# A new order of every engine's calls in the block loop of a fused attention and expert kernel

## The reference

```
nq = layernorm(x)
q, k, v = nq @ wq + bq, ctx @ wk + bk, ctx @ wv + bv          # per head
out = (q @ k.T / sqrt(8)) @ v                                # = q @ (k.T @ v) / sqrt(8)
x = x + softmax(out, axis=-1) @ wo.T + wo_b                   # softmax over the 8 of a head
t = rms_norm(layernorm(x)) * norm_w
probs = softmax(t @ gate.T);  top 2 of 8 experts, weights normalised
h1 = t @ w1.T + 2 * (t @ a1.T) @ b1.T                         # a1, b1, ... are the expert's
h3 = t @ w3.T + 2 * (t @ a3.T) @ b3.T
act = silu(h1) * h3
x = x + sum_e weight_e * (act @ w2.T + 2 * (act @ a2.T) @ b2.T)
```

## Time and profile before

| | |
|---|---|
| time of 3 runs, median (lowest to highest) | 325.44 us (325.40 to 326.32) |
| the profiled execution: time, and its span | 322.72 us, 320.9 us |
| granted TensorE clock over the span | 0.992 of full speed |
| busy share: PE, PEld, DVE, ACT, POOL | 92%, 74%, 73%, 59%, 59% |
| HBM read, written | 12.07 MB, 2.14 MB |

### The profile page before, as it was taken

One profiled execution on the slowest core, in us unless ns is written; L12 is line 12 of the kernel. 1 busy time (PEld: TensorE's weight loads), 2 busy tenths in 40 slices (PEclk: granted clock), 3 DMA queues, 4 the chain that ended last, 5 costly groups with the idle time before them and its releaser, 6 DMA issues.

```text
span 320.9 us, 4516 instructions
## 1 busy us (share of the span) xinstructions
PE 294.3 (92%) x1485; PEld 237.1 (74%) x1485; DVE 233.7 (73%) x621; ACT 187.9 (59%) x309; POOL 188.5 (59%) x171
## 2 busy tenths in 40 slices
PE   6768999879999999999999999999999979996993
PEld 5545778658788778878788778878888767885782
DVE  3879877695679766895679767895579766973364
ACT  2456956358657577448657576548647455654511
POOL 3472469727981589527981689527941688136910
PEclk9999999999999999999999999999999999999996
DMA  5720020200201021200211020200010000200000
GB/s 166 260 66 2 1 67 0 100 0 3 98 21 79 0 66 35 99 0 5 96 30 72 0 65 35 99 1 0 35 66 35 0 1 34 102 0 0 33 2 33
DMA packets 7223, 14.50 MB, mean 45 GB/s; under 512 B 1824, under 2 KB 3104, under 8 KB 7200
## 3 DMA queue, kind: packets, MB, share of 16 engines
q1 hardware_dynamic: 6624, 13.62, 12.7%
q10 hardware_dynamic: 576, 0.59, 0.6%
HBM read 12.07 MB, written 2.14 MB: 44 GB/s over the span
## 4 chain that ended last, share of the span: by engine, by line
PE 35%; DVE 24%; POOL 23%; issue 12%; ACT 2%; DMA 2%; ACTq 0%; DVEq 0%; POOLq 0%
PE h_ps L617 15%; PE h_ps L603 6%; POOL um_lo L1608 5%; POOL heads L1601 4%; POOL v_lo L1623 3%; POOL masks L1614 3%; POOL v L1619 3%; DVE act_first L1315 3%; DVE z_lo L1325 3%; DVE scaled L1307 2%; PE odd_ps L692 2%; DVE masks L1239 2%; PE even_ps L452 2%; PE z_ps L452 2%; PE b_ps L452 2%
## 5 line engine op out<-in xcount | busy, mean ns | idle before, releaser
L617 PE MATMUL h_ps<-um_lo,b_hi 128*128 128x512 f32 x128 | 50.9, 398 | 2.3 <-DVE um_lo L1288 2.1
L961 ACT ACTIVATE silu<-h_ps 128x512 f32<-128x512 f32 x64 | 38.2, 597 | 24.7 <-PE h_ps L617 23.3
L617 PE MATMUL h_ps<-um_hi,b_hi 128*128 128x512 f32 x128 | 51.1, 399 | 1.0 <-DVE act_first L1301 0.9
L617 PE MATMUL h_ps<-um_hi,b_lo 128*128 128x512 f32 x128 | 49.9, 390 | 0.0
L1301 DVE TENSOR_TENSOR act_first<-silu,h_ps 128x512 f32<-128x512 f32 x32 | 21.9, 686 | 36.5 <-ACT silu L961 25.2
L1601 POOL TENSOR_TENSOR heads<-e_o,rec_o 128x512 f32<-128x512 f32 (+1 forms) x9 | 14.8, 1642 | 55.9 <-DVE rec_o L1178 55.9
L1630 POOL TENSOR_TENSOR scaled<-act_second,ratio 128x512 f32<-128x512 f32 x24 | 31.0, 1291 | 11.0 <-DVE act_second L1301 10.9
L1301 DVE TENSOR_TENSOR act_second<-silu,h_ps 128x512 f32<-128x512 f32 x32 | 21.6, 679 | 16.9 <-PE h_ps L617 13.4
L617 PEld LDWEIGHTS h_ps<-um_lo,b_hi 128*128 128x128 f32 x128 | 24.0, 188 | 10.4 <-DVE um_lo L1288 4.6
L953 ACT CAST um_hi<-umf 128x1024 fp32r<-128x1024 f32 x14 | 14.7, 1053 | 28.3 <-DVE umf L1282 28.3
L603 PE MATMUL h_ps<-t_hi,w_hi 128*128 128x512 f32 x64 | 28.5, 446 | 0.9 <-DVE e_o L1171 0.3
(11 more groups left out here) (275 smaller groups left out, 788.4 us busy)
## 6 DMA issues: line engine op xcount, KB each, us to landing
chosen<-choice_dram SPq DMA_DIRECT2D x7, 768.0 KB, 3.9
x_in<-in_x_dram SPq DMA_DIRECT2D x7, 256.0 KB, 2.9
ctx_in<-in_ctx_t_dram SPq DMA_DIRECT2D x7, 256.0 KB, 3.2
out_dram<-y SPq DMA_DIRECT2D x7, 256.0 KB, 2.0
act_second<-in_hidden_w_dram SPq DMA_DIRECT2D x1, 512.0 KB, 4.3
act_second<-in_lora_w_dram SPq DMA_DIRECT2D x1, 512.0 KB, 5.1
v_parts<-in_down_w_dram SPq DMA_DIRECT2D x1, 512.0 KB, 6.1
attn_sb<-in_attn_w_dram SPq DMA_DIRECT2D x1, 260.5 KB, 5.1
```

The lines of the kernel that those rows point to most:

```text
L617: mm = nc.tensor.matmul((h1_ps, h3_ps)[s][n % 2][:], b13[w][:, s, c * P:(c + 1) * P], um[k][m][:, s, :], start=False, stop=(i == 2), skip_ ...
L961: nc.scalar.activation(silu[:, n % SILU_RING, :], h1_ps[n % 2][:], ACT.Silu).then_inc(silu_done.sem, 1)
```

## The change

The change gives the four engine lists of the loop a new order. The lists ahead of the loop and behind it stay, as do all calls, their waits, and SP's list. One constant goes with it: the first of the `w2_product` calls in a loop iteration is now that of quarter 1, since it is the one that clears the bank.

The diff of the loop, in the order PE, ACT, DVE, POOL:

```diff
-W2_ORDER = (0, 1, 2, 3)
+W2_ORDER = (1, 0, 2, 3)
...
                 hidden(b, 0)
+                hidden(b, 1)
                 turn_heads(b + 1)
-                hidden(b, 1)
+                hidden(b, 2)
                 project(b + 1)
-                if early:
-                    turn_x(b + 2)
-                hidden(b, 2)
+                hidden(b, 3)
                 if early:
                     keys_values(b + 2, 0)
+                    turn_x(b + 2)
                 b2_product(b - 1)
-                hidden(b, 3)
+                hidden(b, 4)
+                if early:
+                    queries(b + 2)
+                tail(b - 1)
                 if early:
                     keys_values(b + 2, 1)
-                    queries(b + 2)
-                tail(b - 1)
-                hidden(b, 4)
                 turn_tok(b + 1)
+                hidden(b, 5, (1,))
                 if early:
                     keys_times_values(b + 2)
+                gate(b + 1)
                 hidden(b, 5, (0,))
-                gate(b + 1)
                 if early:
                     attention_out(b + 2)
-                hidden(b, 5, (1,))
                 hidden(b, 6)
                 hidden(b, 7)
+                lora_in(b + 1, 0)
+                w2_product(b, 1)
+                w2_product(b, 0)
                 a2_product(b, 0, 1)
+                a2_product(b, 1, 1)
+                a2_product(b, 2, 1)
                 a2_product(b, 0, 0)
-                a2_product(b, 1, 1)
+                lora_in(b + 1, 1)
                 a2_product(b, 1, 0)
-                w2_product(b, 0)
-                w2_product(b, 1)
-                lora_in(b + 1, 0)
-                lora_in(b + 1, 1)
-                a2_product(b, 2, 1)
                 a2_product(b, 2, 0)
                 w2_product(b, 2)
-                a2_product(b, 3, 1)
                 a2_product(b, 3, 0)
                 w2_product(b, 3)
+                a2_product(b, 3, 1)
...
                 silu_step(b, 0)
+                silu_step(b, 1)
                 heads_turned(b + 1)
+                v_high(b - 1)
+                silu_step(b, 2)
                 if early:
                     normal_x(b + 2)
-                silu_step(b, 1)
-                v_high(b - 1)
+                silu_step(b, 3)
                 if early:
                     x_turned(b + 2)
-                silu_step(b, 2)
+                b_high(b, 0)
                 output_t(b - 1)
-                silu_step(b, 3)
                 normal_tok(b + 1)
+                silu_step(b, 4)
                 if early:
                     queries(b + 2)
-                b_high(b, 0)
-                silu_step(b, 4)
                 tok_turned(b + 1)
...
                 b_high(b, 1)
+                if early:
+                    exp_o(b + 2)
                 b_high(b, 2)
                 z_high(b, 1)
                 z_high(b, 2)
-                exp_gap(b + 1)
-                exp_ratio(b + 1)
-                if early:
-                    exp_o(b + 2)
                 um_high(b + 1, 0)
                 um_high(b + 1, 1)
+                exp_ratio(b + 1)
+                exp_gap(b + 1)
...
                 act_step(b, 0)
                 act_step(b, 1)
+                act_step(b, 2)
                 residual(b + 1)
                 moments_x1(b + 1)
-                act_step(b, 2)
+                act_step(b, 3)
+                if b + 3 < BLOCKS:
+                    moments_x(b + 3)
                 if early:
                     keys_values(b + 2, 0)
-                act_step(b, 3)
+                finish(b - 1)
                 if early:
                     keys_values(b + 2, 1)
-                finish(b - 1)
-                if b + 3 < BLOCKS:
-                    moments_x(b + 3)
+                    mask_ktv(b + 2)
+                tok_low(b + 1)
                 act_step(b, 4)
-                tok_low(b + 1)
-                if early:
-                    mask_ktv(b + 2)
                 top_logits(b + 1)
                 choose(b + 1)
-                act_step(b, 5)
                 if early:
                     top_of_o(b + 2)
+                act_step(b, 5)
+                act_step(b, 6)
+                if early:
                     shift_o(b + 2)
-                act_step(b, 6)
                 act_step(b, 7)
+                b_low(b, 1)
                 scale_last(b)
                 total(b, 2)
                 total(b, 3)
-                b_low(b, 1)
+                mask(b + 1, 0)
+                z_low(b, 1)
                 b_low(b, 2)
-                z_low(b, 1)
                 z_low(b, 2)
-                mask(b + 1, 0)
+                mask(b + 1, 1)
                 mask_u(b + 1, 0)
-                mask(b + 1, 1)
+                mask_u(b + 1, 1)
+                um_low(b + 1)
                 if early:
                     sum_exp(b + 2)
-                um_low(b + 1)
-                mask_u(b + 1, 1)
-                first_weight(b + 1)
                 v_part(b, 0)
                 v_part(b, 1)
+                first_weight(b + 1)
...
+                v_sum(b - 1)
                 scale_mask(b)
-                v_sum(b - 1)
                 v_low(b - 1)
+                scale_step(b, 0)
                 rstd_x1(b + 1)
-                scale_step(b, 0)
                 scale_step(b, 1)
+                b_low(b)
                 total_first(b)
-                b_low(b)
                 z_low(b)
                 if b + 3 < BLOCKS:
-                    rstd_x(b + 3)
                     ctx_low(b + 3)
                 scale_step(b, 2)
+                if b + 3 < BLOCKS:
+                    rstd_x(b + 3)
+                um_low(b + 1)
                 if early:
                     norm_heads(b + 2)
-                um_low(b + 1)
```

## The result

The changed kernel takes 313.85 us (median of 4 runs, 312.93 to 314.08) against 325.42 us (4 runs, 325.16 to 326.32) in the same comparison: a ratio of 0.9634, 95% interval 0.9608 to 0.9661. The profiled execution took 314.08 us, with a span of 312.3 us.

A forecast was written before the change was run, and what follows sets the result against it. PE was taken as the bound, busy 92% of the span. Gains of 5.6 us up to X of block 6, 1.7 in block 6 and 1.2 in block 7, together 8.6, gave 325.44 - 8.6 = 316.8 us, range 314.8 to 322.0.

The forecast's parts named there:

- PE alone, without waits, needs 34.7 us, between 34.5 and 34.9: PE's time per loop iteration, X (third product of hidden step 0) to X: 35.89 - 1.20 + 0.2 - 0.2 us.
- the three waits of 1.20 us: PE's idle times per iteration before X, behind X and before b2_product, 1.20 us together, predicted to go.
- The +0.2 for two more places with a slow first product: On PE, two more groups of small products alone between hidden steps, about 0.1 us each per iteration.
- The -0.2 for slow starts: On PE, slower products behind the waits, predicted to be recovered: up to 0.2 us each, 0.2 per iteration in the sum.
- the new wait at 1.0 us and the late chain at 0.5: Block 6 losses: turn_tok waits about 1.0 us for the normalised tokens; DVE's chain is late by 0.5 us.
- The base: The profiled execution, 322.72 us before, would take 314.1; the median of runs stood 2.72 us above it.
- DVE's chain: On DVE, from key-value product through choice and attention maximum to um_lo, ending 34.7 us behind X, level with PE.
- Rival 1: In blocks 1 to 4 DVE's cast of the choice loses to POOL's ctx_lo, 1.2 us later: 321.4 us, chance 0.26.
- Rival 2: Small POOL operations, rstd_x's root, also hold DVE, 1.0 us in each of blocks 1 to 4: 320.8 us, chance 0.05.
- Rival 3: Blocks 1 to 4: POOL's z_lo holds the choice's subtraction, ctx_lo its cast, 3.65 us each block: 331.4 us, chance 0.08.
- Rival 4: Banks or the choice's DMA hold every iteration at 35.9 us, so nothing changes: 325 us, chance 0.07.
- The other edits cost nothing if their cover holds: Moves such as POOL's um_low ahead of norm_heads add no PE wait, except possibly up to 0.1 us at turn_heads.

The follow-up runs named there:

- best: Changed kernel with the new order carried into the first and the last block: 311.38 us, ratio 0.9572 to the kernel before.
- pool_um: Changed kernel with, in POOL's loop list, norm_heads back ahead of um_low and scale_mask back ahead of v_sum: 324.81 us.
- ctx_early: Changed kernel with one ACT call moved, ctx_high ahead of silu step 5, so that POOL's ctx_lo can start earlier: 317.74 us.
- pool_rstd: Changed kernel with POOL's small rstd_x operations back in their old place ahead of ctx_low in the loop: 316.45 us.
- undo_dve: Changed kernel with DVE's old list in the loop: 338.39 us.
- pool_scale: Changed kernel with one pair of POOL calls in the old order, rstd_x1 ahead of the first scale_step, in the loop: 322.33 us.
- undo_pool: Changed kernel with POOL's old list in the loop: 325.04 us, ratio 1.0014 to the kernel before.
- pool_rstd2: The same kernel as pool_rstd measured again, beside the changed kernel: 315.12 us against 314.3.

## Why the prediction was wrong, point by point

**The step that failed is "PE alone, without waits, needs 34.7 us, between 34.5 and 34.9".** PE alone needs 34.34 us. The mechanism was right: the three waits of 1.20 us went, as I had said. A term of the sum was mis-sized. The +0.2 for two more places with a slow first product came to nothing, since their number stayed the same. The -0.2 for slow starts was -0.12. And I had left out what small groups cost each other side by side, a net -0.23 here: three that were parted gained 0.38, two that got a new neighbour lost 0.15. PE before:

```profile
148.61 1.05 PE L452 MATMUL even_ps<-wo_sb,heads_t 128*128 128x128 f32 x8
149.61 0.63 PE L447 MATMUL z_ps<-query_sb,xn 128*128 128x128 f32 x4
150.00 0.49 PE L617 MATMUL h_ps<-um_hi,b_hi 128*128 128x512 f32 x1
```

And after:

```profile
149.19 1.05 PE L452 MATMUL even_ps<-wo_sb,heads_t 128*128 128x128 f32 x8
150.00 0.48 PE L617 MATMUL h_ps<-um_hi,b_hi 128*128 128x512 f32 x1
...
152.18 0.60 PE L447 MATMUL z_ps<-query_sb,xn 128*128 128x128 f32 x4
152.53 0.48 PE L692 MATMUL odd_ps<-v_hi,b_hi 128*128 128x512 f32 x1
```

Counted from start to start, `project` and `turn_x` took 1.00 + 0.39 us together and 0.81 + 0.35 apart: 0.23 us less. `attention_out` and `turn_tok` gave 0.08 and 0.07 us in the same way. The first hidden product behind a small group is 0.1 us late in either case, and there are five such places in both orders; the second keys, now behind `tail`, cost 0.08 and `keys_times_values` 0.07 more. With the 0.12 us of the slow product behind X that makes 0.35 us, from 34.69 to 34.34. The rows of the first pair were in the trace that I had; I took a flat rate where they gave a price for each pair.

**What it was worth.** Four iterations at 0.36 us, 0.26 in block 1, and 0.42 in block 6, where I also had the new wait at 1.0 us and the late chain at 0.5 (as distances of starts they are 0.89 and 0.38): 2.1 us. Block 7 gave 1.5 us instead of 1.2. Together 10.93 us in loop and end instead of 8.5, of which I had made 8.6. With 0.6 us of the start (below) that is the whole miss.

**The base.** I said that the profiled execution would take 314.1 us, and it took 314.08. That is chance. The start ate 2.33 us of the 10.93: the first hidden product came at 30.30 us before and at 33.41 after, with the same code ahead of it. In the fourteen traces it comes between 30.24 and 37.01 us. From the 48th hidden product on the way to X of block 1 is 24.16 to 24.20 us in all of them except `best` (23.26). In the first 24 us the granted clock was 1.00 in the four traces where it came first (30.24 to 32.63 us), 0.93 or 0.86 in the eight from 33.31 to 35.30, and 0.82 and 0.83 in the last two (36.66 and 37.01); what makes one of the other is not shown. So the trace of before had one of the quickest starts, and my 2.72 us between it and the median belonged to that one execution. On medians the gain is 11.57 us: 10.93, and 0.6 that I put down to these starts without having shown it.

**DVE's chain** was right in its sum: `um_lo` ended at 34.19 us behind X, 0.17 before the next X. I had 34.7, and PE would have waited a little. The key-value product ended at 17.94 us behind X instead of 18.2, the maximum over the attention started at 21.29 instead of 21.8, and from there it was 12.9 us, as forecast. The 0.2 us for `b_lo` beside POOL's `scaled` was not paid (0.68 us).

**Rival 1** named the right race, but the two sides of its sum each left out the key-value product's own time. Behind that product's issue (159.90 us) the subtraction came 4.14 us and `ctx_lo` 4.55, where I had 3.4 and 3.65. The two omissions nearly cancelled, which is luck. The cast won by 0.23 us instead of less than 0.1; in `pool_um` it lost, and in `ctx_early` the subtraction was caught in its place. **Rival 2** is out: `pool_rstd`. **Rival 3** did not happen here, but it does in `undo_dve` and `pool_scale`. My price for it, 3.65 us, was too high for both, since the subtraction is only held for what is left of `z_lo`: 0.66 + 1.05 us in `pool_scale`, 1.2 + 1.1 in `undo_dve`. **Rival 4**: no.

**"The other edits cost nothing if their cover holds"** was true as a sentence and hid the main point. POOL's list takes its long operations out of the way of DVE's chain. Without it all is lost (`undo_pool`, 325.04 us). The pieces don't add: 8.0 us (`pool_scale`), 10.5 (`pool_um`) and 0.8 (`pool_rstd2`) against the 314.3 us of the changed kernel, and 11 for all, because the first two push `z_lo` and `ctx_lo` into the same collision with the choice, and with all of them back the cast goes free.
